# Writing out all hardware loops of a mixture-of-experts and attention block

## The reference, cut to what matters

```python
x = x + 0.5 * ffn(layernorm(x), ...)     # 32 experts, 6 per token, one shared expert
x = x + attn(layernorm(x), ...)          # 64-token segments, 8 heads, and segment means
x = x + 0.5 * ffn(layernorm(x), ...)

def ffn(x, ...):
    scores = sigmoid(x @ gate_weight.T)
    # best 4 of 8 groups, then best 6 experts, weights normalised and times 2.5
    # routed = sum over chosen experts of weight * (silu(x @ g.T) * (x @ u.T)) @ down.T
    return routed + (silu(x @ shared_g.T) * (x @ shared_u.T)) @ shared_down.T
```

## Time and profile before

| | us |
|---|---|
| runs without a profile | 1800.16, 1805.71, 1810.05 (median 1805.71) |
| the profiled execution's own time | 1813.27 |
| its span, first to last instruction | 1811.4 |
| PE busy | 1367.3 (75%) |
| PE weight loads busy | 1141.0 (63%) |
| DVE busy | 1035.4 (57%) |
| POOL busy | 897.4 (50%) |
| ACT busy | 716.7 (40%) |
| mean granted TensorE clock | 0.874 of full |

### The profile page before, as it was taken

How to read it: one execution, slowest core, us unless ns; L and a number is a source line. 1 busy time by engine, 2 the same in 40 slices (tenths; PEclk the granted TensorE clock), 3 DMA queues, 4 the chain that set the end, 5 groups by cost and what they waited for, 6 DMA issues and landing times.

```text
span 1811.4 us, 47211 instructions
## 1 busy us (share of the span) xinstructions
PE 1367.3 (75%) x10480; PEld 1141.0 (63%) x10481; DVE 1035.4 (57%) x5308; ACT 716.7 (40%) x2232; POOL 897.4 (50%) x949
## 2 busy tenths in 40 slices
PE   6556655388888888879988888871878778787985
PEld 5445554377777777468666666641777777776664
DVE  6444553456556565557466666655555555555575
ACT  2222221155555555500455555430555555555300
POOL 4565556245444444422035555565345444444586
PEclk9666666599999999999888888855999999999998
DMA  9852223244444554387012222234444444544597
GB/s 321 293 198 94 98 101 111 82 149 148 142 149 148 161 164 148 108 298 260 8 64 102 102 98 98 103 114 158 136 138 152 142 145 139 181 146 130 180 303 249
DMA packets 154769, 274.52 MB, mean 152 GB/s; under 512 B 27942, under 2 KB 107067, under 8 KB 154688
## 3 DMA queue, kind: packets, MB, share of 16 engines
q1 hardware_dynamic: 116288, 160.27, 29.2%
q0 software_dynamic: 38400, 113.31, 16.9%
HBM read 146.59 MB, written 131.07 MB: 153 GB/s over the span
## 4 chain that ended last, share of the span: by engine, by line
PE 31%; issue 5%; DVE 4%; ACT 3%; DMA 3%; another core or an unknown queue 2%; POOL 1%; ACTq 1%; SPq 0%; DVEq 0%; POOLq 0%
PE ps L781 27%; DMA ans<-answers 3%; PE ps L904 3%; ACT xbt L1376 1%; ACT ans L1504 1%; POOL xres L763 1%; ACTq L1404 1%; PE ps L789 1%; DVE yb L2018 0%; PE ps L923 0%; DVE smax L2098 0%; DMA blk<-normed_transposed 0%; ACT xnt L1328 0%; DVE prob L2108 0%
## 5 line engine op out<-in xcount | busy, mean ns | idle before, releaser
L781 PE MATMUL ps<-xbt,ans 128*128 128x128 f32 x3072 | 422.7, 281 | 140.5 <-ACT xbt L1376 133.2
L781 PEld LDWEIGHTS ps<-xbt,ans 128*128 128x128 f32 x3072 | 380.5, 195 | 165.6 <-ACT ans L1386 122.2
L742 POOL DMA_INDIRECT answers<-yb,didx x208 | 204.5, 983 | 245.6 <-DVE yb L1896 180.1
L742 POOL DMA_INDIRECT answers<-ans,didx x208 | 204.4, 983 | 226.8 <-DVE ans L1896 152.5
L726 POOL DMA_INDIRECT dispatch_rows<-blk,idx x192 | 196.3, 1022 | 209.3 <-issue 116.7
L1886 DVE TENSOR_TENSOR hb<-ps,sg 128x128 f32<-128x128 f32 x416 | 120.6, 290 | 274.3 <-ACT sg L1396 176.7
L1386 ACT COPY ans<-wgu 128x512 f32 x416 | 255.6, 614 | 0.5 <-issue 0.5
L702 POOL DMA_INDIRECT dispatch_rows<-blk,idx x192 | 186.6, 972 | 139.4 <-issue 57.0
L1396 ACT ACTIVATE sg<-ps 128x128 f32<-128x128 f32 x416 | 115.8, 278 | 353.2 <-PE ps L781 306.4
L781 PE MATMUL ps<-wdn,hb 128*128 x768 | 232.3, 385 | 0.0
L1875 DVE SCALAR_TENSOR_TENSOR picked<-iota_e,etab,blk 128x32 f32<-128x32 f32 x832 | 177.0, 250 | 87.2 <-issue 34.2
(11 more groups left out here) (282 smaller groups left out, 2305.3 us busy)
## 6 DMA issues: line engine op xcount, KB each, us to landing
blk<-dispatch_rows SPq DMA_DIRECT2D x384, 160.0 KB
ans<-answers SPq DMA_DIRECT2D x54, 512.0 KB, 5.0
ans<-answers SPq DMA_DIRECT2D x54, 256.0 KB, 4.9
wgu<-in_gate_up SPq DMA_DIRECT2D x32, 256.0 KB
dispatch_rows<-blk,idx POOLq DMA_INDIRECT x384
dispatch_rows<-padt SPq DMA_DIRECT2D x32, 160.0 KB
blk<-dispatch_rows SPq DMA_DIRECT2D x64, 80.0 KB
yb<-answers SPq DMA_DIRECT2D x10, 512.0 KB, 4.8
```

The costliest lines, as they stand in the source:

```text
L742: pool.indirect_dma_start(out=answers_dram, out_offset=bass.IndirectOffsetOnAxis(ap=didx[:, q:q + 1], axis=0), in_=block_answers(q), in_of ...
L781: return nc.tensor.matmul(out_, lhs, rhs, start=start, stop=stop)
```

## The change

Every hardware loop becomes a loop of the Python program that builds the kernel, so each turn is written out with constants. The bodies, their order and their waits stay the same. `Steps.rebase`, which carried DVE's own step count across a loop, is no longer needed. SP's weight loads in route 1 were in a loop too.

```diff
 def by_pairs(eng, n, body):
-    body(0, 0)
-    body(1, 1)
-    with eng.Fori(1, n // 2) as pair:
-        body(pair * 2, 0)
-        body(pair * 2 + 1, 1)
+    for i in range(n):
+        body(i, i % 2)
...
 def pairs_by_two(eng, body, last):
-    body(0, 0)
-    body(1, 1)
-    with eng.Fori(1, NT // 4 - 1) as g:
-        body(g * 2, 0)
-        body(g * 2 + 1, 1)
-    for p in range(NT // 2 - 2, last):
+    for p in range(last):
         body(p, p % 2)
...
         def pool_experts(pool, s):
-            with pool.Fori(0, NB // ANSWERS) as g:
+            for g in range(NB // ANSWERS):
...
         def pe_experts_run(pe, s):
             step = pe_experts(pe, s)
-            for n in range(8):
-                step(n, n, m=0)
-            with pe.Fori(1, (WHOLE - MIXED) // 8) as g:
-                for q in range(8):
-                    step(g * 8 + q, q)
-            for n in range(WHOLE - MIXED, NB + 2):
+            for n in range(NB + 2):
                 step(n, n % 8, m=0)
...
         def v_pairs(v, st, body, last, steps, rest=2):
-            body(0, 0)
-            body(1, 1)
-            start = st.base + st.n
-            groups = (NT // 2 - rest) // 2
-            with v.Fori(1, groups) as g:
-                st.rebase(g * steps + (start - steps))
-                for k in range(2):
-                    body(g * 2 + k, k)
-                assert st.n == steps, (st.n, steps)
-            st.rebase(start + (groups - 1) * steps)
-            for p in range(2 * groups, last):
+            for p in range(last):
                 body(p, p % 2)
...
-            for n in range(16):
-                step(n, n % 8, m=0)
-            with v.Fori(2, WHOLE // 8 - 1) as g:
-                for q in range(8):
-                    st.rebase(g * 8 + (start + q - 2))
-                    step(g * 8 + q, q)
-            st.rebase(start + WHOLE - 8 - 2)
-            for n in range(WHOLE - 8, NB + 2):
+            for n in range(NB + 2):
                 step(n, n % 8, m=0)
```

More of the change, by code:

```diff
@@ L491, in load_experts @@
             assert E == NT
-            if isinstance(p, int):
+            if p == 0:
                 sp.wait_ge(consts, N_CONST)
@@ L515, in pair @@
                         store(p * 2 + j, j)
-            pair(0)
-            with sp.Fori(1, NT // 2) as p:
+            for p in range(NT // 2):
                 pair(p)
@@ L569, in sp_experts @@
             fetch(first[0], 0)
-            for n in range(LOADS):
-                load(n, n, m=0)
             peeled = 2 * DOWNS + (MIXED - DOWNS) + 2 * MIXED
[L573 to L576, removed]
+            for n in range(WHOLE):
                 load(n, n % LOADS, m=0)
                 k = n - (WHOLE - peeled)
+                if k < 0:
+                    continue
                 if k < 2 * DOWNS:
@@ L1416, in act_experts @@
             act.reg_load(expert[0], itab[0:1, 2:3])
[L1417 to L1422, removed]
+            for n in range(NB):
                 step(n, n % 4, m=0)
```

## The result

The changed kernel took 1835.51 us (1828.33 to 1839.89) against 1805.71 before: a ratio of 1.013 with a 95% interval of 1.008 to 1.018. The forecast was 1793 in a range up to 1823, so the sign was wrong and the time lies outside the range. The profiled execution took 1839.89 us (span 1838.0).

The account below looks back on a forecast made before the run. No engine is full over a stage; route 1's cycle is POOL's, with idle gaps. Route 1 10, attention 3, the rest 0 make 13 us off 1805.7: 1793 us, range 1770 to 1823.

Parts of the forecast that it names:

- Route 1, -10 us: POOL's cycle in route 1: six odd-to-even passages in the loop save 1.68 us each, 10 us; bounds 0 and 12.
- the 6.60 us: POOL's two stops at written-out pair 14 of route 1, 3.47 + 3.13 us, expected to remain in each turn.
- the 1.68: Saving per route 1 turn: POOL's stops fall from 8.28 to 6.60 us, 1.28 table load and 0.4 register work.
- My own sign of being wrong: The prediction is wrong if route 1's odd-to-even wait goes or grows, or the blocks' pace moves over 0.04 us.
- Rival A: Route 1: earlier scatter bursts only starve ACT and PE earlier and longer; nothing lands, about 1803 us; chance 0.24.
- Rival B: Expert stages slow to their written-out ends' pace as code packets and scatters share DMA engines: +34, about 1827 us; chance 0.19.
- Rival C: Route 1: ACT's 17.63 and PE's 11.36 us waits could be the branch itself; far faster, about 1750 us; chance 0.10.
- Attention, -3 us: Attention: five DVE turns save 2.5 us (between 0 and 4.9), PE's and ACT's six branches 0.5: 3 us.
- the 0.74 us: Attention: DVE's piece from slots to `idx`, 3.36 us looped against 2.62 written out; 0.41 of it may be a norm.
- Experts, 0: Expert stages: written-out blocks show no sign of a gain; taken as 0, bounds 34 us loss and 37 us gain.
- The 0.04 us: Expert stages: the prediction is wrong if the blocks' pace moves by more than this either way.
- Code to load, 0: Whole kernel: loading the added code costs 0; if not hidden, its price is inside the experts' loss bound.

Follow-up runs that it names:

- gate_on_silu: All loops written out, plus POOL waiting for the next pair's SiLU before a pair's ninth scatter, against the kernel before: 0.990; repeated in a slow session 0.987.
- r1_all_written: The kernel before with only the loops of route 1 written out, on all five engines: 1477.4 us against 1477.4, ratio 1.000.
- gate_before: The kernel before, all loops kept, plus POOL's wait for the next pair's SiLU before the ninth scatter: 1479.9 us against 1476.4, ratio 1.001.
- gate_before_2: The kernel before, loops kept, with POOL's wait for the next pair's SiLU, repeated in a slow session: 1827.4 us against 1839.2, ratio 0.995.
- all_written: The changed kernel run once more, all loops written out, against the kernel before: 1858.5 us against 1845.5, ratio 1.011.

## Why the prediction was wrong, by its own steps

**Route 1, -10 us: the step that failed.** It measured +28.7, and its bounds had no room for a loss. The saving at the table load was read rightly: all 16 table loads at the SiLU's line lost their idle time. ACT's groups of the changed kernel:

```profile
L1336 ACT ACT_TABLE_LOAD x16 | 20.5, 1283 | 0.3
...
L1336 ACT ACTIVATE ssg<-ps 128x256 f32<-128x256 f32 x32 | 11.8, 383 | 216.4 <-remote 159.9 <-PE ps L766 38.6 <-issue 17.5
```

The trace before had 92.4 us of idle time before these loads and 91.9 before the SiLUs, 184.3 together; now it is 216.7, on the SiLUs alone. What failed is the sentence that the 6.60 us stay and the 1.68 go. I took POOL's two stops for a sum of work, from which one can subtract. They were an order: ACT's wait for PE ended inside the first stop (250.37, 2.8 us after the burst), and the four scatters behind that stop ran beside the others' catching up. With the additional wait the stops are 4.00 + 2.80 = 6.80 us, where I had 6.60; the turn goes from 39.4 to 37.7 us, 1.7 where I had worked out 1.68, and route 1 from 313.6 to 305.8 us, -7.8 where I had -10. That the two turns differ by just 1.7 is in part luck, since the 39.4 is a mean over unequal turns. Nor does any run show the 0.4 us of register work in my 1.68: what they show is the loads' idle time and the turn, 37.7 us. The gain that I had read is there; it is only worth having while the order stands. My own sign of being wrong, that the odd-to-even wait goes or grows, came: ACT's wait went from 17.63 to 21.70 us, PE's from 11.36 to 17.27.

**Rival A** named the right mechanism, scatters that starve the others, and set its price at 10 us of lost gain. I let the burst begin earlier and didn't ask what the next wait would do when its event came earlier too: it is the wait for the choice (`sel`) that ends the burst. The trace before showed how close it was: the choice came at 250.85, 3.3 us after POOL's burst, and DVE's steps inside the burst were slow (from `ex` to `sel` 239.00 to 250.85, 11.9 us; 3.8 us in the calm trace, 169.24 to 173.07; 7.8 us after). A few of these slow steps earlier, and the choice falls inside the burst.

**Rival B** had the right sign, slower, and for the wrong reason: it put the loss on the experts and their code packets, which cost nothing that shows. Its 1827 us also lay outside my own upper bound of 1823. **Rival C** did not come: ACT's wait stayed in written-out code.

**Attention, -3 us.** The piece from slots to `idx` is 2.9 us in what had been the loop's pairs, as forecast (2.6 to 3.0), 3.4 before, and 2.6 where no norm stands in it: of the 0.74 us 0.44 were to be had, and 0.3 were the norm. No run shows the 0.5 us for PE's and ACT's branches; the runs show only the stage as a whole. `smax` follows after a longer wait for PE, as the earlier trace rows had it for pair 13:

```profile
1115.35 0.23 DVE L1627 TENSOR_TENSOR slot<-ps,base 128x64 f32<-128x64 f32 x1 [0.94 <-PE ps L766]
1118.00 0.29 DVE L1660 MAX8 idx<-slotm 128x8 int32<-128x32 f32 x2
1118.72 0.69 DVE L2056 TENSOR_REDUCE smax<-ps 128x8 f32<-128x512 f32 x1 [0.44 <-PE ps L766]
```

The stage took 377.9 us here (375.6 before). Over the held traces, loops have 375.6, 381.5, 385.7 and 377.3, written out 377.9, 374.5 and 372.0: means of 380.0 and 374.8. The two ranges overlap, so these 5 us are not clear of the spread. In calm sessions it is most of what writing out gains (the change itself was not run in one): the stage has 291.2 to 301.3 us with loops and 282.9 to 290.2 written out, and a pair goes from some 16.4 us to 15.4, close to POOL's own 12 x 1.27 = 15.2 (in gate_on_silu a scatter of this stage, too, mostly follows the last after 0.97 + 0.30 us).

**Experts, 0.** Right. The same blocks as in the long rows, DVE's scaling alone, took 309.40 / 152 = 2.04 and 304.15 / 152 = 2.00 us a block:

```profile
418.75:728.15 309.40, 72.46 (x152) 1.00 0.49 149
1342.95:1647.10 304.15, 72.45 (x152) 1.00 0.50 153
```

Before it was 2.00 and 2.04. The 0.04 us that I had named as a sign of something are no more than the spread between executions.

**Code to load, 0.** Right. In the changed kernel, 100 to 300 us, the code-loading queues, where the earlier trace rows had none:

```profile
q8 instruction: 5, 0.08, 0.2%
q14 instruction: 8, 0.07, 0.1%
```

That is 0.15 MB in 200 us; over the whole execution the two queues went from 33 and 48 packets to 91 and 135. In calm sessions route 1 took 241.8 us written out (r1_all_written) and 243.5 in loops (gate_before). So the waits that rival C put down to the branch itself come without a move of code: the looped route 1 moved no code packet from 100 to 300 us, and in calm sessions it loses only 1.7 us over six turns. These traces can't say what a turn would cost if its code had to be loaded again.

## What to carry to other kernels

Before subtracting a saving from a cycle, ask which wait bounds the stretch in which the others are held up, and whether the saving moves that wait's event across it. Here ACT's long wait ended at 250.37 and the choice came at 250.85; with two events so close the order can tip, and a saving of 1.7 us a turn became a loss of 3.7. Where a long run of one engine's issues starves the others, as POOL's scatters did here, pace it by an event of the engine that is starved (the SiLU: 0.987 held, against 1.011 without that wait), not by one of an engine that happens to be on time. And compare kernels within a session: the written-out code gained 1% in one condition of the machine (all but route 1 written out, 0.987 to 0.992) and lost 1% in the other (the change, 1.011 and 1.013).

## What the runs showed of the hardware

- One kernel, unchanged, took 1477 us in some sessions and 1842 in others, on one chip too. Scatters took 0.97 us and ACT's copies of the expert weights 0.61 us in both; some matmuls were longer in the held traces, those of the attention above all (128x256 of `xbt` and `wil`: 561 ns on average in before, 411 in gate_before), where the granted clock was 0.84 (before, 905 to 1190 us) against 0.95 (gate_before, 739 to 959 us). The large difference is how late the other engines went on while POOL issued indirect transfers: 16.5 us behind the gate-up matmuls (the change) against 1.2 (r1_all_written). In one trace PE's own matmuls came late too (gate_before_2, up to 2.44 us apart), so it was not only ACT's and DVE's waits for others that ended late. A turn of route 1 took 39.5 us (before) or 30.7 (gate_before), an expert block 2.04 or 1.55. Why was not found.
- In the held condition ACT's wait for PE ended 2.8 to 3.0 us after POOL's last scatter where POOL then stopped, after a burst of 16 (before, 247.58 to 250.37; all_written, 96.62 to 99.48) and after one of 20 (the change, 231.28 to 234.31). Where POOL went on after 2.80 us it ended 4.2 us after the burst (all_written, 178.76 to 182.98).
- With ACT's loop in place (before), its table load at the passages from an odd to an even pair came only after the SiLU's wait: 92.4 us of idle time before the 16 loads, nearly all before six of them. Written out (the change), it was done at once: 0.3 us before all 16.
